# The last piece of a decoder's first attention moved by one and two steps of its step tables, and an earlier choice of second experts

## The reference

```python
x = _layernorm(x + attn(x))     # keys, values, exp(key_att/16), cumulative sums over the sequence
x = _layernorm(x + xattn(x, ctx_1024, ctx_1024, mask))   # 16 heads of 16, 77 keys
x = _layernorm(x + ffn(x))      # 8 experts of 256-1024-256, the best 2 of a row, weighed by softmax

# attn
h = _layer_norm(hidden_states, gamma, beta)
keys = h @ Wk.T + bk;  values = h @ Wv.T + bv
key_att = keys @ Wka.T + bka
keys_weight = exp(key_att / sqrt(d_model))
keys_weight = keys_weight / cumsum(keys_weight, axis=1)
return cumsum(keys_weight * keys, axis=1) * values

# ffn, the choice of experts
logits = flat @ router_w.T + router_b
topk_vals, topk_idx = top_k(logits, 2)
topk_w = softmax(topk_vals, axis=-1)
```

## Time and profile before

| what | value |
|---|---|
| median of 3 runs | 512.8 us (512.52 to 514.48) |
| the profiled execution | 510.51 us |
| its span | 508.8 us |
| granted TensorE clock, mean | 0.993 |
| attention steps 0 to 63 | about 24 to 206 us of the span |
| expert tiles | from there to 500 us |

### The profile page before, as it was taken

One profiled execution on the slowest core, in us unless ns is written; L12 is line 12 of the kernel. 1 busy time (PEld: TensorE's weight loads), 2 busy tenths in 40 slices (PEclk: granted clock), 3 DMA queues, 4 the chain that ended last, 5 costly groups with the idle time before them and its releaser, 6 DMA issues.

```text
span 508.8 us, 10956 instructions
## 1 busy us (share of the span) xinstructions
PE 488.2 (96%) x3302; PEld 440.3 (87%) x3302; DVE 358.1 (70%) x1034; ACT 266.3 (52%) x879; POOL 266.3 (52%) x409
## 2 busy tenths in 40 slices
PE   6999999999999999999999999999999999999990
PEld 6778787888888888999989999999999999999990
DVE  4988596686768986347876776766666666666674
ACT  4776777585867777553343344334433443344320
POOL 4424342233222524155567776776666766766566
PEclk9999999999999999999999999999999999999997
DMA  8149731745565744475356676665566566756420
GB/s 231 23 141 352 248 95 48 267 153 177 168 224 170 246 143 181 136 239 190 116 181 234 215 237 214 232 215 181 205 220 231 189 208 219 247 198 205 146 53 1
DMA packets 57536, 93.84 MB, mean 184 GB/s; under 512 B 12143, under 2 KB 49273, under 8 KB 52359
## 3 DMA queue, kind: packets, MB, share of 16 engines
q1 hardware_dynamic: 50231, 80.05, 46.5%
q0 software_dynamic: 5616, 12.82, 8.5%
q10 hardware_dynamic: 1632, 0.27, 0.3%
HBM read 65.64 MB, written 30.32 MB: 189 GB/s over the span
## 4 chain that ended last, share of the span: by engine, by line
PE 35%; DVE 20%; issue 17%; POOL 17%; DMA 6%; ACT 2%; POOLq 1%; DVEq 0%; SPq 0%; ACTq 0%
PE psum_b L1652 7%; PE psum_v L1788 5%; PE psum_a L1753 5%; DMA work<-weighed_outputs,routing 5%; POOL routing L806 4%; POOL out L815 4%; DVE routing L1509 3%; PE psum_m L1806 3%; POOL work L797 2%; POOL work L802 2%; POOL front_then_w_ring L760 2%; PE psum_c L1774 2%; DVE work L1523 2%; DVE work L1525 2%; PE psum_b L1907 1%
## 5 line engine op out<-in xcount | busy, mean ns | idle before, releaser
L1051 ACT ACTIVATE front_then_w_ring<-psum_b,front_then_w_ring 128x128 f32<-128x128 f32 x160 | 45.6, 369 | 75.4 <-PE psum_b L1907 71.7
L1051 ACT ACTIVATE front_then_w_ring<-psum_a,front_then_w_ring 128x128 f32<-128x128 f32 x152 | 43.2, 368 | 71.1 <-PE psum_a L1907 68.5
L1907 PEld LDWEIGHTS psum_b<-front_then_w_ring 128*128 128x128 f32 x640 | 74.6, 192 | 0.9
L1907 PE MATMUL psum_b<-front_then_w_ring 128*128 128x128 f32 x640 | 75.1, 275 | 0.0
L1932 PE MATMUL psum_v<-expert_w,front_then_w_ring 128*128 x320 | 72.6, 379 | 0.2 <-issue 0.2
L1907 PEld LDWEIGHTS psum_a<-front_then_w_ring 128*128 128x128 f32 x608 | 70.9, 192 | 0.9
L1907 PE MATMUL psum_a<-front_then_w_ring 128*128 128x128 f32 x608 | 71.2, 275 | 0.0
L1932 PE MATMUL psum_c<-expert_w,front_then_w_ring 128*128 x304 | 69.0, 379 | 0.0
L934 ACT ACTIVATE work<-psum_a,score_max 128x77 f32<-128x77 f32 x256 | 62.2, 335 | 11.7 <-DVE score_max L1240 11.4
L1932 PEld LDWEIGHTS psum_v<-expert_w,front_then_w_ring 128*128 128x128 f32 x320 | 59.3, 190 | 7.7 <-issue 0.4
L1932 PEld LDWEIGHTS psum_c<-expert_w,front_then_w_ring 128*128 128x128 f32 x304 | 56.2, 190 | 6.8
(11 more groups left out here) (262 smaller groups left out, 879.0 us busy)
## 6 DMA issues: line engine op xcount, KB each, us to landing
front_then_w_ring<-in_w1b SPq DMA_DIRECT2D x39, 1028.0 KB
weighed_outputs<-routing SPq DMA_DIRECT2D x16, 1024.0 KB, 6.2
expert_w<-in_w SPq DMA_DIRECT2D x8, 1024.0 KB, 11.0
weighed_outputs<-work SPq DMA_DIRECT2D x37, 128.0 KB, 2.0
token_rows<-front_then_w_ring SPq DMA_DIRECT2D x16, 128.0 KB
token_rows<-routing SPq DMA_DIRECT2D x1, 1152.0 KB, 5.4
second_buffers<-in_x SPq DMA_DIRECT2D x4, 256.0 KB, 4.6
front_weights_then_tail<-in_b SPq DMA_DIRECT2D x1, 1024.0 KB, 9.2
```

The source lines that it names most:

```text
L1051: last = act.activation(hidT[t % 2][:, c, :], src[:, n, q * P:(q + 1) * P], ACT.Gelu, bias=bias[:, c:c + 1])
L1907: last = pe.matmul(dst[:, n, q * P:(q + 1) * P], w1[:, k, c * P:(c + 1) * P], xtT[t % 2][:, k, :], start=(k == 0), stop=(k == KD - 1))
```

## The change

The stages of piece 8: "attention" goes from step 45 to 46, "add" from 47 to 48, "x1" from 48 to 49, "x1_turn" from 49 to 50, "queries" from 50 to 51. DVE's `second_choice(0)` and POOL's `weigh(0)` go from step 48 to 47. Nothing is added or removed, and each engine has as many instructions as before.

```diff
-LATE_OF_LAST = ("add", "x1", "x1_turn", "queries")
+LATE_OF_LAST = {"attention": 1, "add": 2, "x1": 2, "x1_turn": 2, "queries": 2}
...
-    late = 1 if p == NP - 1 and stage in LATE_OF_LAST else 0
+    late = LATE_OF_LAST.get(stage, 0) if p == NP - 1 else 0
...
-                if H == RANKS_STEP - 2:
+                if H == RANKS_STEP - 3:
                     weigh(0)
...
-                if H == RANKS_STEP - 2:
+                if H == RANKS_STEP - 3:
                     second_choice(0)
```

## The result

| | median | runs | ratio to before |
|---|---|---|---|
| before | 512.48 us | 7 (510.44 to 514.48) | |
| changed | 517.22 us | 7 (513.67 to 518.34) | 1.0092 [1.0068, 1.0117] |

The change makes the kernel 4.7 us slower. Forecast were +1.4 us and a range up to 515.8. The profiled execution of the changed kernel took 513.67 us, the shortest of the seven, at a mean granted clock of 0.992. The six others took 516.5 to 518.3, at 0.984 to 0.987.

What follows compares the result with a forecast made beforehand. PE was taken to bound the kernel, busy 232.53 of 236 us from 264 to 500 us. A new wait of 2.13 less a gain of 0.73 gave +1.4 us on 512.8: 514.2 us, range 512.0 to 515.8.

Steps and rivals of the forecast that it cites:

- The wait that goes: Step 45 on PE: L1696 no longer waits for DVE's L1179 once moved to step 46, a gain of 0.73 us.
- DVE: Steps 47 to 49: second_choice ahead of the residual, its difference at 170.89, the variance of piece 8 at 173.8.
- POOL: The deciding step: weigh(0) ahead of x1_rsqrt, queue free at 175.69, 1.9 us after the variance; root done at 176.93.
- ACT: L968 waits for POOL from about 175.7 to 176.96, so the exponentials of step 50 start at 177.94.
- PE: Arrives at step 50's turned probabilities at 176.84, starts at 178.97, a new wait of 2.13 us.
- The sum of +1.4 us: PE's new wait at step 50 less the gain at L1696: 2.13 - 0.73 = +1.4 us.
- rival B: POOL does not hold x1; ACT's own order makes PE wait 0.9 us: +0.2 us; with neighbours down to -0.7, chance 0.2.
- costs nothing: All else: later queries, ACT's evictions, DMAs, and PE's clock after a 2 us wait; at most 0.3 us if slack is gone.
- C: POOL's queue ahead of x1: three powers each stretched by 0.45 us, PE waits 1.35 longer, +2.8 us; chance 0.13.
- D: L1696's wait stays, or PE's loss comes back in a later shrinking wait: +1.4 to +2.1 or +0.8; chance 0.05.
- The rule weighed: DVE instructions with two SBUF inputs and GpSimd SBUF reads exclude each other: L1364 against x1_rsqrt, at most 0.22, sum +1.6.

## Why the prediction was wrong

**The wait that goes, DVE, POOL, ACT, PE.** The path is right at every engine. POOL's L700 was walked as 170.97 and came at 172.53 - 1.57 = 170.96; L624 175.69 and 175.67; L968 176.96 and 176.97; the exponentials 177.94 and 177.97; PE 178.97 and 178.97. The sum of +1.4 us is 1.45 in the trace, and rival B, run by itself, was +0.2 for 0.16. Two terms of the sum were a little large, by nearly the same amount. The gain is 0.62 and not 0.73: L1769 of step 46 starts 0.25 behind L1756 (169.88 to 170.13), where 0.14 is the spacing without a wait. And the wait costs 180.54 - 178.40 - 0.14 = 2.00 and not 2.13. That they cancel is no luck, because ACT alone sets when PE goes on, so an earlier PE only waits longer. Nothing of it came back later: PE is 3.02 late behind step 52 and 3.00 at its end.

**The step that failed** is the sentence "A wait of 2 us is too short to lower PE's clock as far as rows tell: PE was busy for 18.88 of the first 24 us at a granted clock of 1.00". It took a row that can't carry it. The windows show 1.00 for these 24 us, but in the first of them PE runs at half speed until 7.0 us, which the matmuls' spacing tells and the column doesn't. The only wait over 1.0 us in those 24, 2.82 us at the very start, lies ahead of that rise; the steps in the middle of the kernel had none over 1.0 us to judge by. So the price of a 2 us wait of PE wasn't bounded from above: it is 3.3 us more in 12 of the 16 executions of the changed kernel. I had it under "costs nothing", and it should have been a rival with a price worked out from a stretch at half clock.

The Trainium skill, "TensorE: Matmul & The Clock Gate", section "HAM oscillation — how this bites in real kernels", describes a kernel whose PE waits about 3 to 5 us for a DMA again and again and works throttled after every such wait. The runs agree that a stretch at the low clock can follow a wait, with 1.86 us of idling and 3.31 us lost after it, but here the waits are shorter than the ones it names. The prediction left that rule out, and read by its figures alone it would not have priced a wait of 2 us either.

**The rivals.** C had the right side (+2.8 us) for a wrong reason: POOL's powers took 1.50 and 1.51 as before, nothing was stretched. D did not occur. The rule weighed changed nothing: in the changed kernel L1364 took its 0.22 us at 177.35, beside `x1_rsqrt`, whose L624 took 0.25 for 0.23.

**What stays open.** Why 1.49 us brought the clock down in six of six and 1.63, some 4 us earlier in the order, in four of twelve; the place in the order and the chip both differ between these two runs, and no run tells them apart. And which part of the spread of 1 to 5 us between executions of one kernel at one clock is the start (profiled: the clock rose at 6 to 15 us, up to 2.8 us late) and which the DMA wait: each is shown in a trace, its share isn't.

## What to carry to other kernels

On an engine as full as this PE a wait costs its own length and perhaps a stretch at half clock behind it. Here that made more than three times the price (4.8 us for 1.45) in the executions that had it, and waits of 0.3 to 0.95 us were free of it in all but at most one of 44 executions. So price the longest single wait and not the sum of waits, and when a step is moved look at what it is queued behind on every engine: moving seven small POOL instructions ahead of three others made the wait, and moving them behind it took the whole loss away. One profiled execution may be the lucky one; compare its time and mean clock with those of the others before explaining a ratio by it.

## What the runs showed of the hardware

The clock did not fall during the wait but 1.0 to 1.6 us after PE had gone back to work (by the partly low stretches of the three traces that have it), stayed at 1.2 GHz for 6.8 us in two traces and 10.2 in a third although PE was busy through it, and this in some executions of the same program and not in others. With matmuls that nobody reads in the wait, the clock stayed up in 38 of 38 executions, by the four traces and by the mean clock (0.990 to 0.994) of the others. POOL's two powers on seven values a partition took 1.50 and 1.51 us beside DVE's residual and moments of piece 8, as they had (1.49 and 1.51) beside its work on the scores and ranks.
